# Marking the padding ids one tile ahead of their store in a graph-attention and expert kernel

## What is computed

```python
def reference(x, adj, ...):
    x = x + gnn(layernorm(x), adj, ...)
    return x + ffn(layernorm(x), ...)

def ffn(x, Wg, bg, W1, b1, W2, b2):
    _, idx = top_k(x @ Wg + bg, 2)
    mask = one_hot(idx, 8).sum(axis=-2)
    h = gelu(einsum('td,edh->teh', x, W1) + b1, approximate=False)
    y = einsum('teh,ehd->ted', h, W2) + b2
    return einsum('ted,te->td', y, mask)
```

## Time and profile before

| what | us |
|---|---|
| median of 3 runs (757.6 to 760.57) | 759.71 |
| the profiled execution, its own time | 758.38 |
| its span in the trace | 756.7 |
| PE busy in it | 689.9 (91%) |
| DVE busy | 599.9 (79%) |
| GpSimd busy | 583.8 (77%) |
| ACT busy | 502.8 (66%) |

### The profile page before, as it was taken

The page is one execution under the profiler, slowest core; times in us unless marked ns, Lnnn a source line. Parts: engine busy times, 40 slices in busy tenths (PEclk is TensorE's granted clock), DMA queues, the critical chain, the costliest instruction groups (busy, mean ns, idle before and its releaser), DMA issues.

```text
span 756.7 us, 17027 instructions
## 1 busy us (share of the span) xinstructions
PE 689.9 (91%) x5408; PEld 357.1 (47%) x5408; DVE 599.9 (79%) x1301; ACT 502.8 (66%) x1017; POOL 583.8 (77%) x685
## 2 busy tenths in 40 slices
PE   5888999999999999999999999998899999999930
PEld 2322233333333333333333333232798999999830
DVE  3788989999999999999999999998977555554410
ACT  4755577786777877777777776665865666666610
POOL 7649596988989889898898988989777755555553
PEclk9998999999999999999999999999999999999975
DMA  7630010011010111101110001051513523233300
GB/s 269 184 107 29 0 30 15 15 43 43 29 45 15 43 43 30 43 15 43 43 29 29 20 26 43 15 141 37 142 52 109 144 79 90 75 91 89 94 13 0
DMA packets 47958, 45.42 MB, mean 60 GB/s; under 512 B 6981, under 2 KB 42576, under 8 KB 47872
## 3 DMA queue, kind: packets, MB, share of 16 engines
q1 hardware_dynamic: 41888, 31.60, 14.7%
q0 software_dynamic: 5984, 12.74, 4.8%
HBM read 27.73 MB, written 18.34 MB: 61 GB/s over the span
## 4 chain that ended last, share of the span: by engine, by line
PE 67%; DVE 14%; issue 8%; ACT 5%; POOL 3%; DVEq 1%; SPq 0%; DMA 0%; POOLq 0%; ACTq 0%
PE scores_ps L453 16%; PE ctx_ps L465 11%; PE z_ps L472 9%; PE scores_ps L622 9%; DVE e L978 9%; PE ctx_ps L648 4%; PE z_ps L648 4%; ACT x_rows L764 3%; PE job_ps L492 2%; PE job_ps L501 2%; PE job_ps L528 2%; PE job_ps L557 2%; POOL out L1477 1%; PE job_ps L513 1%; PE job_ps L484 1%
## 5 line engine op out<-in xcount | busy, mean ns | idle before, releaser
L759 ACT ACTIVATE e<-e 128x2048 f32<-128x2048 f32 x128 | 245.1, 1914 | 145.0 <-DVE e L978 145.0
L978 DVE SCALAR_TENSOR_TENSOR e<-scores_ps,bound_mem 128x2048 f32<-128x2048 f32 x128 | 293.2, 2291 | 33.5 <-PE scores_ps L453 28.6
L1477 POOL DMA_INDIRECT out<-e,near x91 | 92.7, 1018 | 67.7 <-POOL near L1470 32.5
L857 ACT ACTIVATE e<-scores_ps,bound_mem 128x128 f32<-128x128 f32 x364 | 104.0, 372 | 53.0 <-PE scores_ps L622 52.4
L1450 POOL TENSOR_TENSOR ctx_part<-ctx_part,z_inv 128x1024 f32<-128x1024 f32 x60 | 115.8, 1930 | 23.8 <-DVE z_inv L994 23.8
L472 PE MATMUL z_ps<-e,one_column 128*32 128x512 f32 x1024 | 133.4, 592 | 0.0
L1462 POOL TENSOR_TENSOR ctx_sum<-ctx_sum,ctx_part 128x512 f32<-128x512 f32 x90 | 115.4, 1282 | 7.8
L622 PE MATMUL scores_ps<-e,bound_mem 128*128 128x128 f32 x728 | 97.5, 277 | 4.9 <-DVE bound_mem L1174 3.3
L622 PEld LDWEIGHTS scores_ps<-e,bound_mem 128*128 128x128 f32 x728 | 88.5, 192 | 7.8 <-issue 4.4
L986 DVE STREAM_TRANSPOSE ctx_part<-ctx_ps 128x512 f32<-128x512 f32 x128 | 90.3, 705 | 1.8 <-PE ctx_ps L465 1.8
L1424 POOL DMA_INDIRECT sorted_rows<-x_rows,slot x64 | 64.4, 1006 | 18.1 <-issue 16.9
(11 more groups left out here) (182 smaller groups left out, 1001.2 us busy)
## 6 DMA issues: line engine op xcount, KB each, us to landing
near<-sorted_rows SPq DMA_DIRECT2D x91, 130.0 KB, 2.2
near<-in_x SPq DMA_DIRECT2D x16, 256.0 KB, 2.9
bound_mem<-in_adjT SPq DMA_DIRECT2D x4, 1024.0 KB, 9.1
x_post<-in_x SPq DMA_DIRECT2D x16, 256.0 KB, 2.8
sorted_rows<-pad_row SPq DMA_DIRECT2D x1, 3640.0 KB, 15.8
out<-e,near POOLq DMA_INDIRECT x91, 2.7
sorted_rows<-x_rows,slot POOLq DMA_INDIRECT x64, 2.6
bound_mem<-in_w SPq DMA_DIRECT2D x1, 1024.0 KB, 5.6
```

The source lines that it names most:

```text
L759: nc.scalar.activation(every, every, ACT.Exp, scale=SCORE_SCALE).then_inc(exp_done, 1)
L857: nc.scalar.activation(e_flat[:, h_at:h_at + P], scores_ps[:, i % 2, k * P:(k + 1) * P], ACT.Gelu, bias=part_flat[:, bias_at:bias_at + 1]) ...
L978: dve.scalar_tensor_tensor(out=e[:, s % E_RING], in0=scores_ps[:], scalar=-CLIP, in1=to, op0=ALU.max, op1=ALU.min).then_inc(clipped, 1)
L1477: nc.gpsimd.indirect_dma_start(out=out_rows, out_offset=bass.IndirectOffsetOnAxis(ap=near_u[:, id_at:id_at + 1], axis=0), in_=e_flat[:, at ...
```

## The change

The mark of tile `i + 1` now stands ahead of the store of tile `i`, where the mark of tile `i` stood. The waits of `mask_id` and `store` are what they were: the store of a tile still waits for its own mark, which now has one other store and one other mark between itself and that store. The first mark (tile 21) stands ahead of the store of tile 20, and the last two stores have no mark between them. No instruction is added or removed.

```diff
                 while stored < stored_by(k):
-                    if MASKED_AT <= stored:
-                        mask_id(stored)
+                    if MASKED_AT <= stored + 1 < FFN_TILES:
+                        mask_id(stored + 1)
                     store(stored)
                     stored += 1
```

## The result

The changed kernel takes **733.59 us** (median of 4 runs, 733.51 to 735.33) against 760.14 us (median of 4 runs, 757.6 to 761.69) for the one before. The ratio is 0.9659, with a 95% interval of 0.9629 to 0.969. The forecast was 734.7 us in a range of 731.5 to 739. The span of the profiled execution is 731.8 us and its time 733.54 us; the forecasts for these were 731.7 and 733.4.

The account below looks back on a forecast made before the run. GpSimd, waiting for its own marks, was taken to bound the last stage; 3.7 us of PE's stalls and 21.3 us of backlog make 25.0 us off the 759.71 us median: 734.7 us, range 731.5 to 739.

Parts of the forecast that it names:

- GpSimd bound the last stage, not PE: Last stage, tiles 21 to 90: GpSimd needs 2.143 us a tile, the other side 1.897 us, so GpSimd falls behind.
- The wait costs 0.85 us because the preparation comes behind it: Between mark and store: after the wait and MOVE, 0.73 us pass until the store begins; the change removes the 0.85 us.
- The gap that remains: Ahead of each masked store after the change: 0.30 us taken, between 0.16 and 0.49, giving 1.55 us a tile on GpSimd.
- Level at tile 41 (35 to 66): GpSimd's 7.0 us backlog shrinks by 0.35 us a tile, caught up after 20 tiles, ahead of tile 72.
- PE's stalls go, 3.7 us: Tiles 71 to 89: late stores hold back loads and PE waits; 37.85 us should become 34.15 us.
- The end: Last store starts at 722.50 us instead of 747.50; the 9.2 us from there to the span's end stay.
- The new wait for loads: The store of tile i queues behind a mark needing the load of tile i + 1; claimed to cost nothing.
- The stores against DVE's copies: Rival: each store grows by DVE's 0.49 us of weight copies per tile, period 2.04 us, 752.2 us in all; chance 0.05.
- One sign was wrong: Sign: the gap ahead of masked stores falls to 0.16 to 0.49 us, later becoming a true wait for DVE's sum.

Follow-up runs that it names:

- the last pair of runs: One of four second products per tile left out on PE: in the kernel before 757.52 us (ratio 0.9979), in the changed kernel 720.29 us (ratio 0.9481).
- The run with two more additions: Changed kernel with two more mark-sized additions on GpSimd behind each mark, into columns nobody reads: 733.86 us, ratio 0.9667.
- the wait put back: Changed kernel, marks still one tile ahead, but each store also waits for the mark just ahead of it: 760.21 us, ratio 1.001.
- the pairs: Kernel before with marks in twos (mark, mark, store, store), none ahead of its own pair: 732.19 us, ratio 0.9657.
- six more: Changed kernel with six more mark-sized additions on GpSimd behind each mark: 774.38 us, ratio 1.0208.

## Why the prediction was right, point by point

- *GpSimd bound the last stage, not PE.* Shown by the last pair of runs. The chain can't tell: it gave GpSimd 3% before and gives it 4% now, and in the last stretch it still runs along GpSimd's marks and stores. The run with two more additions shows that GpSimd isn't the bound there.
- *The wait costs 0.85 us because the preparation comes behind it.* Shown by the wait put back, which returns gap and time.
- *The gap that remains.* I took 0.30 us between 0.16 and 0.49; it was 0.16, the least. In my rows the 0.16 us stood only behind an operation of 2.15 us; now it stands behind marks of 0.21 to 0.36 us too. The marks were longer than I took (0.301 us for 0.243), and the period came to 1.44 us for 1.55. The time hardly hangs on this: the pairs, at 1.70 us a tile, were level only at tile 68 and lost nothing.
- *Level at tile 41 (35 to 66).* It was tile 37.
- *PE's stalls go, 3.7 us.* Tiles 71 to 89 took 34.02 us, for the 34.15 us worked out without stalls, and the last sum came at 721.25 us for 721.06.
- *The end.* Last store at 722.67 us for 722.50, and the close was 9.1 us for 9.2. The 1.1 us from a sum to its store came out at 1.09.
- *The new wait for loads* cost nothing: the idle time ahead of all 70 marks is 1.1 us together, 1.2 us before.
- *The stores against DVE's copies.* The stores kept 0.998 us, so the rival fell. Once GpSimd is level, the mark begins with DVE's copies (623.90 and 623.91 us) and takes 0.33 us in place of 0.21; that the copies are the cause was not tested. The Trainium skill's rule (SBUF — State Buffer, "Who interferes with whom"), that a VectorE copy in a two-port mode and a GpSimd instruction exclude one another, shows in the marks, if at all.
- *One sign was wrong.* I expected the profile to name DVE's sum as the releaser once GpSimd is level. It names the mark; only sum, MOVE and store side by side show the true one.

## What to carry to other kernels

An engine that waits for its own last instruction can pay more than that instruction: what its sequencer could have prepared meanwhile comes behind it, here on GpSimd 0.85 us ahead of an indirect DMA, for a mark of 0.24. Put between producer and consumer an independent instruction at least as long as the preparation (here a store of 1.00 us against 0.73; a second mark alone hid no more than its own length), or do two producers and then two consumers and pay once for two. More distance gained nothing here. Judge an engine in its stage by its period against the period of its neighbours: GpSimd had 77% in all and 3% of the chain. Yet 0.25 us a tile too much came to 17 us over 69 steps, and about 7 us by which GpSimd was already behind when the marks began could not be made up; together they are nearly all of the 25 us.

## What was not expected of the hardware

- Independent small additions on GpSimd start 0.14 us apart (603.04 and 603.18 us above), although each is shown with a span of 0.18 to 0.45 us in that run. Their spans overlap, and adding them up overstates the work: six more took 1.11 us.
- One store, that of tile 49, has a longer gap ahead of it in both kernels, at different times. Before:

```profile
661.04 1.01 POOL L1477 DMA_INDIRECT out<-e,near  x1 [2.35 <-issue]
```

And after the change:

```profile
647.13 1.01 POOL L1477 DMA_INDIRECT out<-e,near  x1 [2.04 <-DVE e L1192]
```

It goes with the place in the program and not with the time: it stands ahead of tile 49 in all seven kernels without added instructions on GpSimd, between 640.91 and 663.42 us, and ahead of no tile in the two with them. Before, it cost 1.5 us of the path; now GpSimd makes it up. Its cause wasn't tested and stays open.
